# Rows of maxima brought under the queries by single-element transfers through DRAM, in place of a TensorE transpose and a VectorE copy

## The reference, cut to what matters

```python
scores = einsum("bihd,bjhd->bhij", q, k) * scale + lam * (cos and sin parts, same form)
scores = where(causal, scores, -inf)
attn = softmax(scores, axis=-1)
out = einsum("bhij,bjhd->bihd", attn, v)
```

## Time and profile before

| what | value |
|---|---|
| three runs, median (lowest to highest) | 2063.33 us (2060.68 to 2069.52) |
| the profiled execution, its own time | 2052.71 us |
| its span in the trace | 2051.1 us |
| mean granted TensorE clock | 0.921 |
| busy: PE, DVE, ACT, POOL | 85%, 64%, 41%, 18% of the span |

### The profile page before, as it was taken

The page is one execution under the profiler, slowest core; times in us unless marked ns, Lnnn a source line. Parts: engine busy times, 40 slices in busy tenths (PEclk is TensorE's granted clock), DMA queues, the critical chain, the costliest instruction groups (busy, mean ns, idle before and its releaser), DMA issues. The chain is left out here.

```text
span 2051.1 us, 28577 instructions
## 1 busy us (share of the span) xinstructions
PE 1738.7 (85%) x9152; PEld 918.5 (45%) x9153; DVE 1302.5 (64%) x3135; ACT 838.4 (41%) x941; POOL 366.9 (18%) x488
## 2 busy tenths in 40 slices
PE   6999179999999999999999999644429999999954
PEld 3444034444444444444444444134315666666643
DVE  3687577777777777777777775036625555555548
ACT  2677423455555555555555555402202221222211
POOL 0111111121121211112111121103553111111111
PEclk9999568899999999999999999867659999999978
DMA  3454421011020110201102000088521111111143
GB/s 97 144 205 174 176 101 44 7 47 54 7 99 7 54 51 4 99 7 63 43 11 90 7 13 12 11 254 251 201 91 34 46 46 46 46 42 46 44 130 132
DMA packets 99690, 155.57 MB, mean 76 GB/s; under 512 B 10784, under 2 KB 60896, under 8 KB 99200
## 3 DMA queue, kind: packets, MB, share of 16 engines
q1 hardware_dynamic: 85072, 122.66, 18.5%
q0 software_dynamic: 14512, 31.53, 4.3%
HBM read 88.04 MB, written 65.48 MB: 75 GB/s over the span
## 5 line engine op out<-in xcount | busy, mean ns | idle before, releaser
L862 ACT ACTIVATE att_probs<-att_ps_s 128x1024 f32<-128x1024 f32 (+3 forms) x640 | 563.9, 896 | 513.1 <-PE att_ps_s L817 505.8
L817 PE MATMUL att_ps_s<-att_queries,att_keys 49*128 49x512 f32 (+3 forms) x2560 | 628.8, 559 | 21.1 <-ACT att_probs L862 11.6
L876 DVE TENSOR_REDUCE att_maxima<-att_ps_m 128x1 f32<-128x512 f32 x768 | 487.1, 683 | 151.7 <-PE att_ps_m L796 146.6
L796 PE MATMUL att_ps_m<-att_keys,att_queries 48*128 48x512 f32 (+3 forms) x1280 | 502.4, 603 | 43.6 <-DMA att_keys<-k_parts 36.4
L796 PEld LDWEIGHTS att_ps_m<-att_keys,att_queries 48*128 48x128 f32 x1280 | 195.9, 192 | 336.0 <-DVE att_maxima L876 137.6
L879 DVE CUSTOM_DVE_ANT_0 att_ps_m<-att_ps_m,att_future 128x128 f32<-128x128 f32 (+3 forms) x512 | 240.2, 513 | 94.7 <-PE att_ps_m L796 93.4
L817 PEld LDWEIGHTS att_ps_s<-att_queries,att_keys 49*128 49x128 f32 x2560 | 240.2, 190 | 127.8 <-ACT att_probs L862 84.9
L838 PE MATMUL att_ps_o<-att_probs,att_values 128*32 128x512 f32 (+3 forms) x2560 | 269.4, 535 | 11.1 <-POOL att_probs L955 11.1
L1447 PE MATMUL exp_ps_h<-keep_w,exp_rows_t 128*128 x576 | 261.0, 596 | 5.5 <-DVE exp_rows_t L1478 5.5
L1520 ACT ACTIVATE exp_hidden<-exp_product 128x512 f32<-128x512 f32 x72 | 45.4, 631 | 324.8 <-DVE exp_product L1503 324.8
L955 POOL TENSOR_SCALAR_AFFINE_SELECT att_probs<-att_probs 128x512 f32<-128x512 f32 x128 | 81.5, 636 | 489.4 <-ACT att_probs L862 489.3
(11 more groups left out here) (188 smaller groups left out, 1482.4 us busy)
## 6 DMA issues: line engine op xcount, KB each, us to landing
att_queries<-q_parts SPq DMA_DIRECT2D x64, 192.0 KB
att_keys<-k_parts SPq DMA_DIRECT2D x64, 192.0 KB
exp_rows<-sorted_rows SPq DMA_DIRECT2D x72, 129.0 KB, 2.3
v_rows<-pre_v_sb SPq DMA_DIRECT2D x8, 1024.0 KB, 4.4
q_parts<-pre_waves SPq DMA_DIRECT2D x16, 512.0 KB, 3.0
k_parts<-pre_waves SPq DMA_DIRECT2D x16, 512.0 KB, 4.2
att_values<-v_rows SPq DMA_DIRECT2D x32, 256.0 KB, 14.7
out_parts<-att_out_t POOLq DMA_DIRECT2D x32, 256.0 KB, 5.9
```

The costliest lines, as they stand in the source:

```text
L796: pe.matmul(take()[:, 0:width], queries[half, g % 2, c, r, P * q:P * q + P], keys[half, g % 2, k, r, 0:width], start=True, stop=True).then ...
L817: mm = pe.matmul(score_tile(unit, first, last)[:, e], keys[half, g % 2, k // TPC, r, P * (k % TPC):P * (k % TPC) + P].bitcast(F32), querie ...
L862: act.activation(probs[:, step % PROBS, DUO * r:DUO * r + DUO, first:last], score_tile(unit, first, last), ACT.Exp, scale=SCALE).then_inc( ...
L876: dve.tensor_reduce(to, buf[:, 0:width], AX.X, ALU.max).then_inc(s_mr, 1)
```

## The change

The negated maxima are stored to a new DRAM tensor `max_cols` (32 by 128 by 16) as they are, and read back with the axes exchanged, so that each of the 1024 numbers of a row is read by itself. SP issues all three transfers of a chunk, and waits for the store before it issues the two loads. The transpose, the copy, `max_row`, the identity matrix, the ring's bookkeeping and POOL's transfers go; the three `ps_m` tiles serve maxima alone. SP now follows the plan too: it loads quads 0 and 1, then goes through the list, placing rows and starting the loads of quad g + 2 at the last values of quad g. In the plan, `PLACED` becomes 8000 and is counted from VectorE's negation. The list changes with it: the placement event stands directly behind a chunk's last maxima, and ahead of the first scores of its chunk by 31, 25, 16 and 9 units (first to fourth chunk of a quad, from quad 1 on). For chunks 0 to 3 there are 16, 16, 14 and 14 tiles of maxima between, with 0, 0, 0 and 2 units of scores. Behind the loads of quad g + 2 in the list come 7 units, 12 tiles and 3 steps of values, then the placement of chunk 4g + 6, then 16 units until its scores.

```diff
-SWITCH, SEEN, PLACED, SETTLED, EAGER = 200, 200, 2200, 6000, 300
+SWITCH, SEEN, PLACED, SETTLED, EAGER = 200, 200, 8000, 6000, 300
...
-            self.negated_at[n] = self.run("dve", 250, 0) + SEEN // 2
-            self.turns.append(n)
...
-        self.placed_at[n] = self.run("pool", 500, self.slots[-1]) + PLACED
-        self.events.append(("turn_max", n))
+            self.placed_at[n] = self.run("dve", 250, 0) + PLACED
+            self.events.append(("place_max", n))
...
+            def place_max(n):
+
+                g, c = divmod(n, QC)
+                sp.wait_ge(s_neg, n + 1)
+                sp.dma_start(max_cols[n], neg_max[:, n % 2]).then_inc(s_cols, 16)
+                sp.wait_ge(s_cols, 16 * (n + 1))
+                for e in range(DUO):
+                    row = HALF * e + FEAT
+                    sp.dma_start(queries[row:row + 1, g % 2, c].rearrange("p r (q t) -> p (r q) t", q=TPC).bitcast(F32),
+                                 max_cols[n:n + 1, :, DUO * TPC * e:DUO * TPC * (e + 1)].rearrange("o t x -> o x t"),
+                                 allow_slow_non_contiguous=True).then_inc(s_m[c], 16)
+
+            for g in range(2):
+                load_quad(g)
+            for event, *what in plan:
+                if event == "place_max":
+                    place_max(*what)
+                elif event == "values":
+                    g, s = what
+                    if s == STEPS - 1 and g + 2 < QUADS:
+                        load_quad(g + 2)
...
-            def turn_max(n):
-
-                pe.wait_ge(s_neg, n + 1)
-                pe.transpose(take()[0:QUAD * TPC, 0:P], neg_max[:, n % 2], ident[:, :]).then_inc(s_turn, 1)
...
-                    dve.wait_ge(s_turn, n - 1)
+                    dve.wait_ge(s_cols, 16 * (n - 1))
...
-            def keep_row(n, buf):
-                dve.wait_ge(s_turn, n + 1)
-                if n >= 2:
-                    dve.wait_ge(s_m[(n - 2) % QC], 32 * ((n - 2) // QC + 1))
-                dve.tensor_copy(max_row[:, n % 2], buf[0:QUAD * TPC, 0:P]).then_inc(s_row, 1)
...
-            def place_max(n):
-
-                g, c = divmod(n, QC)
-                pool.wait_ge(s_row, n + 1)
-                for e in range(DUO):
-                    row = HALF * e + FEAT
-                    pool.dma_start(queries[row:row + 1, g % 2, c].rearrange("p r t -> p (r t)").bitcast(F32),
-                                   max_row[DUO * TPC * e:DUO * TPC * (e + 1), n % 2]).then_inc(s_m[c], 16)
```

More of the change, by code:

```diff
@@ L547, in __init__ @@
         self.unit = self.value = self.group = 0
-        self.slots, self.turns, self.settling = [], [], []
+        self.slots, self.settling = [], []
         self.exp_at, self.masked_at, self.summed_at = [], {}, []
-        self.kept_at, self.negated_at, self.placed_at = {-1: 0}, {}, {}
+        self.kept_at, self.placed_at = {-1: 0}, {}
     def run(self, engine, ns, ready):
@@ L654, in made @@
         left = 0
-        while self.value < QUADS * STEPS or self.turns or self.group < len(self.groups):
+        while self.value < QUADS * STEPS or self.group < len(self.groups):
             now = self.free["pe"]
@@ L659, in made @@
                 continue
-            scores, values, maxima, turn = self.scores_ready(), self.values_ready(), self.max_ready(), self.turn_ready()
+            scores, values, maxima = self.scores_ready(), self.values_ready(), self.max_ready()
             ripe = sum(self.probs_ready(step) <= now + 300 for step in range(self.value, self.steps_scored()))
@@ L666, in made @@
             left = 0
-            if turn is not None and (turn <= now + EAGER or scores is None and values is None):
-                self.turn()
-            elif maxima is not None and maxima <= now + EAGER:
+            if maxima is not None and maxima <= now + EAGER:
                 self.maxima()
@@ L676, in made @@
                     values = None
-                ready = [(max(at, now), i) for i, at in enumerate((scores, maxima, values, turn)) if at is not None]
-                (self.scores, self.maxima, self.values, self.turn)[min(ready)[1]]()
+                ready = [(max(at, now), i) for i, at in enumerate((scores, maxima, values)) if at is not None]
+                (self.scores, self.maxima, self.values)[min(ready)[1]]()
         while self.settling:
@@ L681, in made, with attend @@
         return self.events
[L684 to L696, removed]
+def attend(nc, q_parts, k_parts, v_rows, out_parts, inv_rows, max_cols):
     plan = Plan().made()
@@ L765, in load_v, with load_quad @@
                              rows_v[chunk_row(g, c), :, :, g % NQ * QUAD * VW:(g % NQ + 1) * QUAD * VW]).then_inc(s_v[g % 2][c], 16)
-            for g in range(QUADS):
+            def load_quad(g):
                 if g >= 2:
@@ L778, in _ @@
             pe.wait_ge(s_const, CONSTS)
-            slots = ring_slots(plan)
+            tiles = [0]
             def take():
[L783 to L786, removed]
+                tile = tiles[0]
+                tiles[0] += 1
+                if tile >= SLOTS_PS:
+                    pe.wait_ge(s_mr, tile - SLOTS_PS + 1)
+                return ps_m[tile % SLOTS_PS]
             def max_tile(n, r, q, k, e):
@@ L849, in _ @@
                     max_tile(*what)
-                elif event == "turn_max":
-                    turn_max(*what)
         @block.scalar
@@ L912, in _ @@
                 if event == "max":
-                    take_max(*what, tile, ps_m[slots.pop(0)[0]])
+                    take_max(*what, tile, ps_m[tile % SLOTS_PS])
                     tile += 1
@@ L916, in _ @@
                         negate(what[0], tile)
-                elif event == "turn_max":
-                    keep_row(*what, ps_m[slots.pop(0)[0]])
                 elif event == "values":
@@ L927, in _ @@
             pool.memset(future[:, :], 0.0).then_inc(s_made, 1)
-            pool.memset(ident[:, :], 0.0).then_inc(s_made, 1)
-            pool.wait_ge(s_made, 3)
+            pool.wait_ge(s_made, 2)
             for i in range(2):
@@ L973, in _ @@
             for event, *what in plan:
-                if event == "turn_max":
-                    place_max(*what)
-                elif event == "scores":
+                if event == "scores":
                     mask(*what)
@@ L1679, in program @@
     prepare(nc, x, Wq, Wk, Wv, Wqp, Wkp, lambda_raw, q_parts, k_parts, v_rows)
-    attend(nc, q_parts, k_parts, v_rows, out_parts, inv_rows)
+    attend(nc, q_parts, k_parts, v_rows, out_parts, inv_rows, scratch("max_cols", [CHUNKS, P, QUAD * TPC]))
     with ExitStack() as stack:
```

10 lines of the change are left out of this document (2 added, 8 removed).

## The result

The changed kernel takes 2335.01 us (median of 4 runs, 2330.13 to 2335.36), the kernel before 2062.01 us in the same series: a ratio of 1.1311, with a 95% interval of 1.1278 to 1.1344. The forecast was 2302 us, with a range of 2200 to 2470. The profiled execution took 2334.9 us with a span of 2333.2, 282.1 us more than the span before.

The account below looks back on a forecast made before the run. PE, taking work in plan order, was held to bound attention, late rows stopping it. Start +85, load stretches +168, last chunks +18, removed -32 make +239 on 2052.7: 2292, plus 10.6 for the median, 2302 us; range 2200 to 2470.

Parts of the forecast that it names:

- What bounds: In attention, PE is busy 122 of 125 us per quad and follows the plan's order; a missing row of maxima stops it.
- At the start: Chunks 0 to 3: first placement waits behind all 40 loads, scores start at 341.6 instead of 267.70; together +85 us.
- At each load stretch: Chunks 6, 10, 14, 18, 22, 26: placement queued behind loads, PE stalls 26 us and 2 for the clock, six times, +168.
- Last chunks: Chunks 7, 11 ... 31: 10.9 us of cover against 12.5 for placement; seven times 1.6 and 1 for restart, +18 us.
- Clock: PE restarts at 0.50 clock after stalls: 2 us for each of four at the start, 2 per load stretch, 1 per last chunk.
- Removed: Attention: 32 transposes and PE's idle time ahead of them, 39.6 us, of which 32 us were taken as saved.
- Sum: Whole kernel: 85 + 168 + 18 - 32 = +239 us on the profiled 2052.7, giving 2292, or 2302 for the median.
- Elements: Each placement's single-element loads: 25 ns an element on eight engines, 6.4 us; 12.5 us from negated maxima to placed.
- The 13 ns and 97 ns: Lower and upper price per element in placement loads, 3.3 and 24.8 us; totals 2252 and 2613 us.
- the store does not pass the loads: Rival at the seven placements behind loads: the store is not held up, each comes 11.5 us earlier, 2222 us; chance 0.18.
- The lead does not cover it: Rival at start and load stretches: the plan's longer lead hides placements, only -32 stays, 2031 us; chance 0.04.
- Elements are not as dear as 60 ns: Rival on placement loads: elements cost 60 ns or more, or their issue is long, 2455 to 2613 us; chance 0.18.

Follow-up runs that it names:

- deferral: Changed kernel, with SP issuing quad 1's loads behind chunk 2's placement and quad g+2's behind chunk 4g+6's, instead of ahead: 2135.25 us, ratio 1.0411.
- POOL's queue: Changed kernel, with POOL instead of SP issuing each placement's store and two element loads, SP keeping only the loads: 2247.67 us, ratio 1.0962.
- the lead that gave next to nothing: Changed kernel with PLACED = 14000 in the plan and nothing else: 2284.34 us, ratio 1.1094.
- The last pair of runs: New q/k layout and SETTLED 12000 in the kernel before, 2028.97 us; the same plus deferred loads and PLACED 14000 in the changed kernel, 2018.00 us.
- the extra pair: Changed kernel with two more element loads per chunk of the same numbers into a spare tile, scores waiting for all four: 2478.43 us, ratio 1.2096.

## Why the prediction was right, step by step

- *What bounds*: right. PE follows the list, and late rows stop it.
- *At the start*: scores at 340.99, forecast 341.6. Chunks 1 to 3 waited 18.0 us, forecast 13.
- *At each load stretch*: forecast 26 us of stall at the six chunks 6 to 26, measured 27.5 on average, at just those. Opening to store was 35.7 to 36.7 us (forecast 35.9), store behind the backlog 14.2 to 14.4 (14), elements 10.3 to 11.8 (9.6). That it is the queue is shown by deferral, by POOL's queue and by the lead that gave next to nothing.
- *Last chunks*: 3.6 us each against 1.6; it is a small difference of two larger numbers.
- *Clock*: after the stall at chunk 6, PE ran at 0.50 from 582 to 586 us and at 0.97 from 586. The forecast has 8 + 12 + 7 = 27 us for it in total, which is too little. Windows over attention, the kernel before and then the changed one (columns as in rows 2):

```profile
...
240.00:1318.00 1078.00, 1017.60 (x6432) 464.26 (x6432) 762.93 (x1919) 563.86 (x640) 173.09 (x289) 0.96 0.12 40
...
240.00:1604.00 1364.00, 1044.09 (x6400) 469.52 (x6400) 755.30 (x1886) 561.72 (x640) 138.68 (x225) 0.86 0.17 32
...
```

Without the transposes' own 9.3 us, the same matmuls took 1044.1 - 1008.3 = 36 us longer. That they ran at a lower clock is the likely cause, and no run separates it.
- *Removed*: this term of the sum was mis-sized. I took 32 of 39.6 us. In these windows PE's idle time grew by 259.5 us while the waits on placed rows grew by 266.3 (272.7 less 6.4), so other idle time shrank by only 7; with the transposes' own 9 that is 16 us. The last pair of runs gave 15. So most of the 30.6 us of idle time ahead of the transposes stayed, in other places.
- *Sum*: forecast 244 us of waits (68 at chunk 0, 8 at chunks 1 to 3, 6 x 26, 7 x 1.6) + 27 for the clock - 32 = +239. Measured in attention 266 + 36 - 16 = +286, and the stages behind it were 4 us shorter: +282. The 43 us missing are 22 of waits (all but chunk 0's too short by 1 to 2 us), 9 of clock and 16 of transposes, less those 4. All three terms erred to the same side. One small slip: for chunks 1 to 3 the prediction's own numbers give 13 - 4.3 = 8.7, not 8.4.
- *Elements*: the price was near in size (12.5 us from negated maxima to placed, and 11.8 from store to scores at chunk 1) and wrong in its parts, so that it came out near is partly luck. The DMA view of 330 to 342 us, and windows (columns as in rows 2) of the first element loads and of the restart at chunk 6:

```profile
...
q1 hardware_dynamic: 2074, 0.01, 21.4%
...
```

```profile
...
334.00:336.00 2.00, 0.00 (x0) 0.00 (x0) 0.00 (x0) 0.00 (x0) 0.00 (x0) 0.50 0.81 1
336.00:341.00 5.00, 0.01 (x2) 0.04 (x2) 0.00 (x0) 0.00 (x0) 0.00 (x0) 0.50 0.00 0
...
582.00:586.00 4.00, 4.00 (x26) 1.72 (x24) 2.15 (x6) 1.02 (x1) 0.00 (x0) 0.50 0.00 0
586.00:590.00 4.00, 3.96 (x21) 1.85 (x19) 3.02 (x5) 2.66 (x3) 1.26 (x2) 0.97 0.21 68
...
```

The engines are busy at 0.81 of all sixteen from 334 to 336, more than half, so it wasn't eight engines with 256 elements each, as I had counted from the eight rows of 128. (The same rule of the Trainium skill, applied to those rows, gives eight as well; here the trace differs from it, or from how I read the shapes, and decides.) 21.4% of 16 times 12 us over 2074 packets is 20 ns for one, against 25; spread over sixteen engines that is 2.6 us in all, where the forecast had 6.4. But hardly any packet is recorded after 336 and the scores start at 341: some 5 us between the last recorded packets and the scores are not in the packets' time, and where they go is open. The 13 ns and 97 ns were bounds of the wrong quantity: by the extra pair, 2048 more elements cost 8.3 us, of which packets' time is a third. The fit of the Trainium skill by which the prediction had 2220 us (DMA: Bandwidth & Descriptors, Anatomy of one DMA) is given there for transfers that POOL issues. SP issued these, and that same run shows a price that the fit lacks.
- *Rivals*: the store does not pass the loads (14.4 us behind them, 1.4 alone). The lead does not cover it. Elements are not as dear as 60 ns. That elements are read singly is shown by over 2000 packets for one pair of loads.

## What to carry to other kernels

When a wait-and-issue pair moves to another queue, read what stands ahead of it there and what will stand behind it: here the first cost 186 us, and on the other queue 208 us of waits went while the time fell by only some 72 us (1.1311 less 1.0962, times 2062). Here more lead in the list of work did not help against a load stretch that lies between issue and use; the place in the queue did. Once nothing waited for it, replacing a transpose by single-element transfers (about 12 us from store to use) came out 0.4% ahead, which is within the measurement's spread: whether it pays is not shown.

## What the runs showed of the hardware that was not expected

- q and k loads ran at 79 to 83 GB/s with 0.2 of the engines busy, and at 210 GB/s with 1.00 once their rows lay at one step. The kernel before became 0.8% slower by this, and 1.6% faster than it had been once VectorE's reciprocal stood later.
- A pair of element loads spread over more than eight of the engines (a mean share of 0.81 from 334 to 336 us), and the scores came some 5 us after its last recorded packets; which part of the chain those 5 us are was not found out.
- Writing single elements to DRAM cost about what reading them did: 12.5 us from store to scores against 11.8.
